# Layer norms taken batch by batch, late tiles moved behind two chunks, and products nobody reads in TensorE's waits

## The reference

```python
x = x + _L0_xattn_ref(_layernorm(x), ctx_1024, ...)   # 16 heads of 128, RMS norms of q and k
x = x + _L0_ffn_ref(_layernorm(x), ...)    # quantized to blocks of 32 with a shared exponent; hidden 1024
x = x + _L1_xattn_ref(_layernorm(x), ctx_1024, ...)   # softmax of q k^T from ctx alone, times x
x = x + _L1_ffn_ref(_layernorm(x), ...)    # silu(gate) * up, hidden 1024, float32
x = x + _L2_xattn_ref(_layernorm(x), ctx_1024, ...)   # 16 heads of 16, per-head norms
x = x + _L2_ffn_ref(_layernorm(x), ...)    # weights looked up in a table of 16
x = x + _L3_xattn_ref(ctx_1024, _layernorm(x), ...)   # 16 states of a scan over ctx, gated by x
x = x + _L3_ffn_ref(_layernorm(x), ...)    # Hadamard transforms around the FFN
```

## Time and profile before

| what | value |
|---|---|
| median of 3 runs | 1023.35 us (1017.09 to 1023.35) |
| the profiled execution | 1021.45 us |
| its span | 1019.6 us |
| PE busy over the span | 871.9 us (86%) |
| DVE / ACT / POOL busy | 691.8 / 544.4 / 364.5 us |

### The profile page before, as it was taken

How to read it: one execution, slowest core, us unless ns; L and a number is a source line. 1 busy time by engine, 2 the same in 40 slices (tenths; PEclk the granted TensorE clock), 3 DMA queues, 4 the chain that set the end, 5 groups by cost and what they waited for, 6 DMA issues and landing times.

```text
span 1019.6 us, 13088 instructions
## 1 busy us (share of the span) xinstructions
PE 871.9 (86%) x4352; PEld 614.5 (60%) x4352; DVE 691.8 (68%) x1369; ACT 544.4 (53%) x1015; POOL 364.5 (36%) x233
## 2 busy tenths in 40 slices
PE   5796899999999999755699886858598899999998
PEld 3364687777877778523345633727487784545646
DVE  4248689999898998788556686756988972353311
ACT  2377677787777778952323461435587672112110
POOL 1211677887787887567341112000000000600000
PEclk8799899999999999977699997958699999999999
DMA  4003000010000000000502000000000001100000
GB/s 127 16 0 139 16 17 16 15 31 15 15 15 15 15 19 6 1 1 1 200 1 84 1 0 1 1 0 2 0 2 1 2 1 71 61 1 1 14 7 21
DMA packets 12924, 24.25 MB, mean 24 GB/s; under 512 B 4280, under 2 KB 8656, under 8 KB 11728
## 3 DMA queue, kind: packets, MB, share of 16 engines
q1 hardware_dynamic: 12448, 20.53, 6.1%
q10 hardware_dynamic: 432, 3.15, 0.8%
HBM read 22.63 MB, written 1.05 MB: 23 GB/s over the span
## 4 chain that ended last, share of the span: by engine, by line
PE 37%; DVE 12%; ACT 5%; issue 4%; POOL 2%; ACTq 0%; DVEq 0%; POOLq 0%
PE PS L2283 14%; PE PS L2295 7%; PE PS L2448 4%; DVE mxf L1707 2%; PE PS L2198 1%; PE PS L2218 1%; PE PS L2149 1%; PE PS L2235 1%; PE PS L1815 1%; PE PS L2432 1%; PE PS L2433 1%; PE PS L2412 1%; PE PS L2102 1%; PE PS L2142 1%; ACT regC L1043 1%
## 5 line engine op out<-in xcount | busy, mean ns | idle before, releaser
L468 POOL TENSOR_SCALAR veps<-mv 128x4 f32<-128x4 f32 x16 | 7.8, 485 | 382.9 <-DVE mv L1115 379.4
L509 POOL TENSOR_TENSOR X<-X,xn 128x512 f32<-128x512 f32 x62 | 104.6, 1687 | 69.7 <-ACT xn L735 69.1
L1219 DVE TENSOR_TENSOR_SCAN regB<-regB 128x1024 f32<-128x1024 f32 x32 | 82.1, 2569 | 0.2
L1199 DVE TENSOR_SCALAR_CACHE_REDUCE regA<-PS,nrq 128x256 bf16<-128x256 f32 x128 | 56.0, 475 | 37.7 <-PE PS L1890 35.9
L759 ACT ACTIVATE regA<-PS,nb,rq 128x256 f32<-128x256 f32 x128 | 72.2, 577 | 10.6 <-DVE regA L1199 9.8
L2448 PE MATMUL PS<-regA 128*128 128x128 f32 x512 | 74.0, 291 | 2.9 <-ACT regA L1058 2.7
L502 POOL TENSOR_TENSOR y<-y,regB 128x1024 f32<-128x1024 f32 x32 | 75.7, 2364 | 0.1
L1912 PE MATMUL PS<-regA 128*128 128x256 f32 x256 | 67.0, 384 | 7.3 <-DVE qss L1186 7.2
L2448 PEld LDWEIGHTS PS<-regA 128*128 128x128 f32 x512 | 67.5, 205 | 6.4 <-ACT regA L1058 5.3
L1921 PE MATMUL PS<-regA 128*128 128x256 f32 x256 | 66.6, 383 | 0.0
L1890 PE MATMUL PS<-regA 128*128 128x256 f32 x256 | 66.4, 382 | 0.0
(11 more groups left out here) (279 smaller groups left out, 2113.5 us busy)
## 6 DMA issues: line engine op xcount, KB each, us to landing
regA<-in_W SPq DMA_DIRECT2D x16, 384.0 KB, 3.1
regB<-in_wg SPq DMA_DIRECT2D x2, 1024.0 KB, 6.3
regB<-in_wu SPq DMA_DIRECT2D x2, 1024.0 KB, 8.3
X<-in_x SPq DMA_DIRECT2D x1, 1024.0 KB, 7.6
regC<-in_wg ACTq DMA_DIRECT2D x1, 1024.0 KB, 6.2
regC<-in_wu ACTq DMA_DIRECT2D x1, 1024.0 KB, 8.1
regC<-in_wd ACTq DMA_DIRECT2D x1, 1024.0 KB, 11.7
regB<-in_wd SPq DMA_DIRECT2D x1, 1024.0 KB, 8.9
```

The costliest lines, as they stand in the source:

```text
L509: pool.tensor_tensor(xt, xt, part, ALU.add).then_inc(x0_add, 1)
L1199: ins = dve.tensor_scalar(spill[:, i, q, :], bank(S_BANK + i)[:, q * S:(q + 1) * S], nrq[par][:, t:t + 1], None, ALU.mult, ALU.min, accum_ ...
L1219: dve.tensor_tensor_scan(v(hs), v(decays), v(dBu), 0.0, ALU.mult, ALU.add).then_inc(scan_done, 1)
```

## The change

- Norms 4 and 5 are taken by batch (`part` 0 and 1, two tiles each) on all four engines. A list, `LN_ORDER`, counts the semaphores. Norm 3 goes to a place of its own (`xn_late`).
- `x_scales(1)`, `x_units(1)` and the rounding stand behind the fourth add on DVE. The whole of tiles 4 to 7 stands behind chunks 0 and 1 of FFN1: `x_transpose(1)` behind chunk 0, gate and up of tile 4 behind chunk 1, of 5, 6 and 7 behind chunks 3, 4 and 5.
- `keep_busy(to, count)` puts matrix products of 512 columns whose result nobody reads into a bank that is free: 30 after the last head, 4 behind the first transposes, 7 before each of the first four hidden transposes, and 36 around the norms by batch: 98 in all.
- FFN1's three weights are loaded one by one, as their places come free: the first two early, the third after the last `state_in`. The last decay lies in regC. The last state's second `state_in`, its scans and its outs stand behind the norms.
- The keys' steps begin later and follow a table, `K_STEPS`: chunk 2 of the second half carries two. Down tiles stand between queries and keys.

The diff, cut to its core:

```diff
...
-D0_BANK = [6, 6, 6, 6, 6, 7, 6, 7]
-X1_BANK = [6, 6, 7, 6]
-dA_last = u3
+D0_BANK = [6, 6, 4, 5, 6, 7, 6, 7]
+X1_BANK = [2, 3, 6, 7]
+dA_last = regC[:, 0:2 * T].rearrange("p (c b l) -> p c b l", c=2, b=B)
+xn_late = regC[:, 4608:4608 + TPH * DIM].rearrange("p (t d) -> p t d", t=TPH)
...
-TRANSPOSED = [0, 1, 4, 5, 6, 7, 8, 9, 10, 11, 13, 15]
+LN_ORDER = [(n, 0) for n in range(4)] + [(4, 0), (4, 1), (5, 0), (5, 1)] + [(n, 0) for n in range(6, 16)]
+TRANSPOSED = [at for at in LN_ORDER if at[0] not in (2, 3, 12, 14)]
...
-def xn_ready(n, t=TPH - 1):
-    if n in ACT_LN:
-        return xn_tile, TPH * (n - 2) + t + 1
-    return ln_xn, n + 1 - (len(ACT_LN) if n > 2 else 0)
-def xn_read(n):
-    if n in TRANSPOSED:
-        return xnT_done, TRANSPOSED.index(n) + 1
-    return (q8_done, QX[n - 2] + 1) if n in (2, 3) else (sx_done, (n - 10) // 2)
+def ln_tiles(n, part=0):
+    return range(2 * part, 2 * part + 2) if n in (4, 5) else range(TPH)
+def ln_count(n, part=0):
+    return LN_ORDER.index((n, part)) + 1
+def xnT_count(n, part=0):
+    return TRANSPOSED.index((n, part)) + 1
+def ln_before(n, part=0):
+    return (n - 1, 1 if n == 6 else part if n == 5 else 0)
+def xn_ready(n, part=0, t=None):
+    if n not in ACT_LN:
+        return ln_xn, n + 1 - (len(ACT_LN) if n > 2 else 0)
+    tiles = ln_tiles(n, part)
+    done = sum(len(ln_tiles(*at)) for at in LN_ORDER[2:LN_ORDER.index((n, part))])
...
+K_STEPS = [(4,), (5,), (6, 7), (8,), (9,), (10,), (11,), (12,)]
...
+    sp.wait_ge(du_done, 1)
+    sp.wait_ge(y_done, 1)
+    sp.dma_start(wf_g, a["wg1"]).then_inc(ld_f1, 16)
+    sp.wait_ge(dA_done, 2 * NST)
+    sp.dma_start(wf_u, a["wu1"]).then_inc(ld_f1, 16)
+    sp.wait_ge(ssm_use, 4 * (NST - 1) + 3)
+    sp.dma_start(wf_d, a["wd1"]).then_inc(ld_f1, 16)
...
-    for tile, name in ((wf_g, "wg1"), (wf_u, "wu1"), (wf_d, "wd1")):
-        sp.dma_start(tile, a[name]).then_inc(ld_f1, 16)
...
-    pool.wait_ge(du_done, 1)
-    pool.wait_ge(y_done, 1)
-    pool.memset(dA_last[:, :, :, 0:1], 0.0).then_inc(zero_set, 1)
...
+    pool.wait_ge(wt_tr, 2)
+    pool.memset(dA_last[:, :, :, 0:1], 0.0).then_inc(zero_set, 1)
...
-    add_out(4 * H0 - 1, 3)
...
+    add_out(4 * H0 - 1, 3)
+    scan_sum(H0 - 2, 0)
...
-    scan_sum(H0 - 2, 0)
...
+    ln_pow(4, 0)
+    ln_pow(4, 1)
+    ln_pow(5, 0)
+    ln_pow(5, 1)
...
-    ln_pow(4)
-    ln_pow(5)
...
-    in_units(TPH)
...
-    hidden(TPH)
-    for tt in range(TPH + 1, NT):
+    for tt in range(TPH, NT):
...
-    ln_apply(3)
+    probs1_scaled(0)
+    silu_pair(1)
...
-    probs1_scaled(0)
-    for tt in range(1, TPH):
+    ln_apply(3)
+    probs1_scaled(1)
+    probs1_out(0)
+    for tt in range(2, TPH):
...
-        if tt >= 2:
-            hidden_out(tt - 2)
+        hidden_out(tt - 2)
...
-    x_out(1)
-    ln_apply(4)
-    ln_out(4)
-    silu_pair(TPH)
-    ln_apply(5)
-    ln_out(5)
-    silu_pair(TPH + 1)
+    for part in range(2):
+        ln_apply(4, part)
+        ln_out(4, part)
+    for part in range(2):
+        ln_apply(5, part)
+        ln_out(5, part)
...
+    act.wait_ge(ssm_use, 4 * NST + 1)
...
-        if c == 1:
+        if c == 0:
+            x_out(1)
+        elif c == 1:
+            silu_pair(TPH)
+        elif c == 3:
+            silu_pair(TPH + 1)
+            hidden_out(TPH)
+        elif c == 4:
...
-            hidden_out(TPH)
-        elif c == 2:
...
+        elif c == 5:
...
-        elif c in (3, 4):
-            hidden_out(TPH + c - 1)
-        elif c == 6:
-            ln_apply(6)
+            hidden_out(TPH + 2)
+    hidden_out(NT - 1)
+    ln_apply(6)
...
+    ln_apply(7)
...
-    ln_apply(7)
-    keys_step(4)
-    keys_step(5)
...
-    keys_step(6)
...
-        keys_step(7 + c)
-        if c == 1:
+        for s in K_STEPS[c]:
+            keys_step(s)
+        if c == 0:
...
-        if c == 4:
-            ln_out(8)
-    keys_step(4 * B - 1)
-    keys_step(4 * B)
-    deviations(B, TPH)
-    keys_step(4 * B + 1)
-    keys_step(4 * B + 2)
+    ln_out(8)
+    for s in range(13, 4 * B + 3):
+        keys_step(s)
+        if s == 15:
+            deviations(B, TPH)
...
-        decays = dA_last if isinstance(n, int) and n == NST - 1 else dA
+        decays = dA
+        if isinstance(n, int) and n == NST - 1:
+            decays = dA_last
+            dve.wait_ge(zero_set, 1)
...
-    layer_norm_stats(3)
...
+    layer_norm_stats(3)
...
-    x_scales(1)
+    state_in(NST - 1, 0)
...
-    x_units(1)
...
-    layer_norm_tiles(4, (0,))
-    state_in(NST - 1, 0)
+    ffn0_add(1)
+    layer_norm_stats(4, 0)
...
+    ffn0_add(2)
+    layer_norm_tiles(4, (2,), 1)
+    ffn0_add(3)
+    link(layer_norm_tiles(4, (3,), 1))
+    layer_norm_mean(4, 1)
+    x_scales(1)
+    attend1_add(0)
+    layer_norm_stats(5, 0)
+    x_units(1)
...
-    ffn0_add(1)
-    layer_norm_tiles(4, (1,))
+    attend1_add(1)
+    layer_norm_stats(5, 1)
...
-    ffn0_add(2)
-    layer_norm_tiles(4, (2,))
-    ffn0_add(3)
-    link(layer_norm_tiles(4, (3,)))
-    layer_norm_mean(4)
+    dve.wait_ge(ln_rstd, ln_count(5, 1))
...
-    attend1_add(0)
-    layer_norm_tiles(5, (0, 1))
-    attend1_add(1)
-    link(layer_norm_tiles(5, (2, 3)))
-    layer_norm_mean(5)
...
-    ffn0_gated(4)
-    state_out(NST - 1, 1)
-    ffn0_round(4)
-    ffn0_gated(5)
+    state_out(NST - 1, 1, W_BANK)
...
+    gate(0, 0, 1)
+    ffn0_gated(4)
+    gate(0, 0, 2)
+    ffn0_round(4)
+    gate(0, 0, 3)
+    ffn0_gated(5)
+    gate(0, 0, 4)
...
-    gate(0, 0, 1)
+    ffn0_add(4)
...
-    gate(0, 0, 2)
-    ffn0_add(4)
+    gate(0, 0, 5)
...
+    ffn0_add(5)
...
-    gate(0, 0, 3)
-    ffn0_add(5)
+    gate(0, 0, 6)
...
-    gate(0, 0, 4)
...
-    gate(0, 0, 5)
+    gate(0, 0, 7)
...
-    gate(0, 0, 6)
+    ffn_add(0, 0, 0)
...
-    gate(0, 0, 7)
-    keys_step(2)
-    ffn_add(0, 0, 0)
+    ffn_add(0, 0, 1)
...
+    keys_step(2)
+    ffn_add(0, 0, 2)
...
-    ffn_add(0, 0, 1)
-    keys_step(4)
-    ffn_add(0, 0, 2)
-    keys_step(5)
...
-    keys_step(6)
...
+    def keep_busy(to, count):
+        for _ in range(count):
+            pe.matmul(bank(to), sel[:, 0, :], bc3[:, 0:HALF], start=True, stop=True)
+    pe.wait_ge(pt_evac, G)
+    keep_busy(PT_BANK, 30)
...
-        if hf:
-            pe.wait_ge(at_out, B)
-        else:
-            pe.wait_ge(exp1, 2)
+        pe.wait_ge(*(xnT_done, xnT_count(5, 1)) if hf else (exp1, 2))
...
+    SLOT_FROM_CHUNK = {8: 1, 9: 2, 10: 3, 11: 4, 12: 5, 15: 6}
...
-            if tt == NT - 2:
-                pe.wait_ge(gated, 1 + nb)
-            elif i == 2 * NT - 2:
-                pe.wait_ge(gated, 3)
+            if i in SLOT_FROM_CHUNK:
+                pe.wait_ge(gated, SLOT_FROM_CHUNK[i])
...
+        elif tt == 1:
+            pe.wait_ge(d0_add, 1)
...
-            pe.wait_ge(d0_add, tt)
-        elif tt == TPH:
-            pe.wait_ge(x1_add, 2)
-        elif tt == TPH + 1:
+            pe.wait_ge(h0_done, 2 * TPH)
+        elif tt < TPH + 2:
...
+    keep_busy(PT_BANK, 4)
...
+    broadcast_state(NST - 1, 1)
...
-    broadcast_state(NST - 1, 1)
...
+    ffn0_down(3)
+    pe.wait_ge(at_out, B)
+    pe.wait_ge(hqT_done, TPH)
+    keep_busy(1, 8)
+    ln_transpose(4, 0)
+    keep_busy(1, 4)
+    pe.wait_ge(xnT_done, xnT_count(4, 0))
+    attend1(0)
+    keep_busy(1, 4)
+    ln_transpose(4, 1)
+    keep_busy(1, 4)
+    pe.wait_ge(xnT_done, xnT_count(4, 1))
+    attend1(1)
+    keep_busy(1, 8)
+    ln_transpose(5, 0)
+    keep_busy(1, 4)
+    ln_transpose(5, 1)
+    keep_busy(1, 4)
...
-    ffn0_down(3)
-    x_transpose(1)
-    ffn0_gate_up(4)
-    pe.wait_ge(hqT_done, TPH)
-    ln_transpose(4)
-    pe.wait_ge(xnT_done, TRANSPOSED.index(4) + 1)
-    pe.wait_ge(d0_add, TPH)
-    attend1(0)
-    pe.wait_ge(x1_add, 1)
-    attend1(1)
-    broadcast_state(NST - 1, 3)
-    ln_transpose(5)
-    ffn0_gate_up(5)
+    pe.wait_ge(d0_add, 2)
+    broadcast_state(NST - 1, 3, W_BANK)
...
-    pe.wait_ge(ssm_use, 4 * NST + 1)
-    pe.wait_ge(xnT_done, TRANSPOSED.index(5) + 1)
+    pe.wait_ge(xnT_done, xnT_count(5, 1))
+    pe.wait_ge(x1_add, 2)
...
-        if c < 2:
-            pe.wait_ge(h0_done, 11 + c)
-        elif c == 2:
-            pe.wait_ge(h0_done, 13)
+        if c == 2:
+            pe.wait_ge(h0_done, 9)
...
+            pe.wait_ge(h0_done, 10)
+        elif c == 4:
+            pe.wait_ge(h0_done, 11)
+        elif c == 5:
+            pe.wait_ge(h0_done, 14)
+        elif c == 6:
+            pe.wait_ge(h0_done, 15)
+        elif c == 7:
...
-        else:
-            pe.wait_ge(gated, c - 1)
...
-        if c == 1:
+        if c == 0:
+            x_transpose(1)
+        elif c == 1:
+            ffn0_gate_up(4)
+        elif c == 3:
+            ffn0_gate_up(5)
+            hidden_transpose(4)
+        elif c == 4:
+            ffn0_down(4)
...
-            hidden_transpose(4)
-        elif c == 2:
-            ffn0_down(4)
...
+        elif c == 5:
+            ffn0_down(5)
...
-        elif c in (3, 4):
-            ffn0_down(c + 2)
```

(70 more changed lines are left out.)

123 lines of the change are left out of this document (71 added, 52 removed).

## The result

The changed kernel takes 1005.49 us (median of 4 runs, 1003.83 to 1008.0) beside 1022.62 for the kernel before (median of 4). The ratio is 0.9846, 95% interval 0.9803 to 0.9889. The forecast was 1003.5, its range 990 to 1018.

A forecast was written before the change was run, and what follows sets the result against it. No engine was full in the first 83 us; a tile-by-tile chain of waits round PE, ACT, DVE and POOL bound it. 1021.45 - 21.3 + 3.2 = 1003.3, predicted as 1003.5, range 990 to 1018.

The forecast's parts named there:

- Term 1: Stretch up to the second FFN's first chunk: it starts at 488.4 instead of 509.75, -21.3 us.
- 477.7 - 7.0 = 470.7: Fourth early down tile's end: 7.0 us of late-half scales and units leave DVE's line ahead of it.
- the 1.7 that I took for the clock: Before the fourth early down tile: net 1.7 us saved by full-clock transposes and first gate and up products.
- The 3.0 for collisions: Ahead of the first chunk: DVE and POOL overlap and collide, adding 3.0 us, 485.4 to 488.4.
- the 1010 by that rule: Shared-port case before the first chunk: five collisions on the path cost 9.6 us, not 3.0; kernel 1010.
- Term 2: From the second FFN's first chunk to the third attention's first scores: 165.8 us instead of 162.6, +3.2.
- the one line of waits: Last hidden tile, keys 0, norms 6 and 7 one behind the other: 6.6 us of waits.
- the tail: End of the stretch before the first scores: DVE's moved keys' steps, copies and transposes leave PE idle 15 us.
- I take -6.4: PE work from first chunk to scores: low-clock time goes, mostly in the last 48.3 us, saving 6.4 us.
- That wait goes: PE's 8.22 us idle beside POOL's mask product vanishes, since PE now has some 11 us of work there.
- The clock of 1.00 from 431 on: Sign of success: granted clock of 1.00 from 431 to 485 us.
- the rival's 26: From 431 to 488 unread products don't hold the clock and stand in the way: 26 us, kernel 1037; chance 0.07.

The follow-up runs named there:

- reordered tail: Changed kernel with POOL's mask product waiting for the second half's maxima, the keys' steps ahead of adds and queries on DVE, ACT's order following: 996.46 us, ratio 0.9752.
- without the guard: Changed kernel without DVE's wait for the last batch's norm power (from POOL) before the last scans: 1007.43 us, ratio 0.985.

## Why the prediction was right, and where its steps were not

The time, the point at which the chunk starts and the mechanism came out. That the median lies only 2 us from the forecast is in part luck: the forecast summed to 1003.3 for the profiled execution, which took 1008.0, and errors of either sign meet in it. The 4.7 come apart like this.

**Term 1** (forecast -21.3, measured -19.4). The step that failed is "477.7 - 7.0 = 470.7", and with it the down tile's end at 469.0: it is 473.66, 4.7 later. The 7.0 us of work left DVE's line, but all together the tile came 4.1 sooner: 0.4 is an earlier entry, 0.7 the products (entry to tile's end 43.6 without them, 42.9 with), and 3.0 is what is left for the work moved (46.6 to 43.6). The rest DVE now waits, for ACT and PE: 1.44, 0.95 and 1.53 ahead of 458.14, 459.78 and 464.94. Moving the quantization alone in the kernel before brought 1.4. The burst of 30 took 8.33 instead of 7.1, because the clock stood at 0.50 from 433 to 435 in the middle of it, so the x transposes came at 439.15, behind 436.87 of before. The clock fell a second time, to 0.50 from 457 to 459, and gate and up of tile 3 took 3.20 (455.91); in the reordered tail's trace they took 1.89, and its down tile is 1.3 sooner after the entry. Of the 1.7 that I took for the clock, the run without products shows 0.7.

From the down tile's end to the issue of the third load I had 11.7 us (469.0 to 480.7) and it was 11.8 (473.66 to 485.46). The load took 4.8 against 4.7 and ended last, as forecast. The 3.0 for collisions was wrong: none stood on this part of the path, and the one ahead of it, POOL's 3.82 at 433.59, ended at 437.41 under the burst. The two errors, +4.7 and -3.0, with 0.2 in the small terms, leave 1.9. That they nearly cancel is luck.

The Trainium skill (SBUF — State Buffer, "SBUF: two separate sides") says that DVE and GpSimd share one pair of ports, and that the first to start holds it for its whole instruction. The trace agrees where both read SBUF: 3.82 for POOL's 1.91 beside a scan at 433.59, and 2.00 for its 0.19 without the guard. It did not reach the path here, so the 1010 by that rule did not come. The same section lets DVE take the pair only with two inputs in SBUF or in a two-port mode. That agrees with the maxima out of PSUM: 0.66 beside the mask product's 7.02.

**Term 2** (forecast +3.2, measured +7.8). The waits came out: PE idles 170.40 - 138.45 = 31.95 against 34. In parts, forecast in brackets: late tiles 5.45 in six waits of 0.55 to 1.56 (5), the one line of waits 2.02 + 1.16 + 1.98 = 5.2 (6.6), the third chunk 4.01 (4.2), norm 8 1.71 (3.3), the tail 9.46 + 0.34 + 5.35 + 0.34 = 15.5 (15). What failed is the term "I take -6.4" for the clock. PE is busy 138.45 against my 131.7. The work moved in is there, 138.45 - 133.78 = 4.7 (I had 4.3), and the clock gave nothing back: 0.91 before and after. The low clock followed the waits; in the last 22.7 us it is 0.63. I had removed the wait by the mask product and with it the low clock of 48 us, and put 15 us of new waits beside it without asking what the clock would do in them. 6.75 too little work and 2.15 too much wait make the 4.6. Half of the 6.75 is not the tail's: 3.4 of it is low clock ahead of the second half (PE busy 67.95 against 64.56 in the reordered tail's trace, for the same 270 products), which some other traces of this order don't have. In the second half even the reordered tail, with 7 us less of waits, gets hardly any clock back: PE is busy 69.9 against 70.5.

**The tail.** "That wait goes" holds for PE at 617 and says too little. The 7.51 on DVE stayed and came out at the end, in a row that names DVE and not POOL. The reordered tail shows its size: 7.9 us from the second half's first chunk to the scores, and a median 9.0 lower.

**The unread products.** I counted on 1.7 us of clock by them, in term 1; the 6.4 of term 2 lie behind the chunk, where none of them stands. Three runs give nothing that can be told from zero: without them the kernel is the same, in the kernel before they bring nothing, in the reordered tail neither. Their clock is real (0.94 against 0.81), but PE has 30 us of waits in that stretch without them, and what the clock saves between waits they cost again by standing in the queue: -0.7 and +1.7 in the one pair of traces, 0.2 saved in all in the other.

**What I did not price.** Without the loads' new places the kernel takes 14.0 us more, and the forecast spoke of them only as a wait that might be added. **After the scores**: 1.8 us less, within the 3 named. It is no gain of the change: the traces of the new order have 345.1 to 347.5 there.

Of the signs named, the chunk (485 to 492), the load just ahead of it, small operations on POOL free of the scans and the idle ahead of late tiles (0.55 to 1.56) came, and PE no longer waits beside the mask product. The clock of 1.00 from 431 on did not come, nor the scores by 656, and the scans still have a POOL operation beside them (6.16; 4.47 in the kernel without the guard). One sign that was named as wrong did come: the clock at 0.50 under unread products. It cost 1.2 us of burst (8.33 against 7.1) and not the rival's 26.

## What to carry to other kernels

Sum idle and busy time of the bounding engine apart, and give the clock back only for waits that vanish, since a new wait can bring its own slow stretch. When an operation of another engine holds an engine that is busy to the end of the stretch, moving the waiter away from it doesn't remove the loss: ask where that engine finishes. A step made earlier is worth only what the next releaser allows, here a load of 1 MB. And before a shift in a trace is put down to an edit, look whether it is there already ahead of the first instruction that the edit touches.

## What the runs showed of the hardware

- The granted clock fell while PE was working: 0.50 from 433 to 435 with PE busy for the whole 2.00 us, in a burst that had begun 2 us before, after 2.42 us of idle. The 30 products took 8.33 us here and 9.84 in the kernel before, against 7.1 at the full clock (30 x 1.89 / 8). The clock came back within the same burst: the transposes behind it took 0.61.
- The clock is not the same from one execution to the next where the code and the waits are. Eleven traces have the new order. Behind the same wait of 2.02 us the 32 down products took 7.17 in four of them and 8.86 in seven; the second half's first chunk, behind 1.97 or 1.98 us of wait, took 3.70 in three and 5.24 to 5.40 in eight.
- POOL's mask product took 7.02 us beside DVE's maxima out of PSUM, which kept their 0.65, where the same product held DVE's SBUF operation for 7.51. So in these runs it mattered what DVE's operation was, a reduction out of PSUM or a product in SBUF, and not only that both were busy.
- A 1 MB load took 4.8 us alone and 4.9, 7.0 and 9.0 as first, second and third of three.
